# Spectra in 64-row tiles over two banks, the first correlation ahead of the second head sums, and three residual sums on TensorE

## What is computed

```python
Qf = jnp.fft.rfft(Q, axis=2)
Kf = jnp.fft.rfft(K, axis=2)
corr = jnp.fft.irfft(Qf * jnp.conj(Kf), n=Lloc, axis=2)
corr_mean = corr.mean(axis=-1)
w, idx = jax.lax.top_k(corr_mean, top_k)
w = jax.nn.softmax(w, axis=-1)
rolled = jnp.take_along_axis(V[:, :, None, :, :], shifted[..., None], axis=3)
out = jnp.einsum('bhk,bhkld->bhld', w, rolled)
return out @ Wo + bo
...
x = x + jnp.tanh(g_xattn[1]) * _L1_xattn_ref(_layernorm(x, axis=-1), ctx_1024, ...)
x = x + jnp.tanh(g_ffn[1]) * _L1_ffn_ref(_layernorm(x, axis=-1), w_gate, w_up, w_down)
```

## Time and profile before

| | us |
|---|---|
| runs | 276.53, 276.31, 274.62 |
| median | 276.31 |
| profiled execution, in all | 276.65 |
| its span (first to last instruction) | 274.8 |
| PE busy | 253.9 (92%) |
| DVE busy | 190.7 (69%) |
| ACT busy | 164.6 (60%) |
| POOL busy | 131.0 (48%) |

### The profile page before, as it was taken

One profiled execution on the slowest core, in us unless ns is written; L12 is line 12 of the kernel. 1 busy time (PEld: TensorE's weight loads), 2 busy tenths in 40 slices (PEclk: granted clock), 3 DMA queues, 4 the chain that ended last, 5 costly groups with the idle time before them and its releaser, 6 DMA issues.

```text
span 274.8 us, 6251 instructions
## 1 busy us (share of the span) xinstructions
PE 253.9 (92%) x2152; PEld 196.4 (71%) x2152; DVE 190.7 (69%) x494; ACT 164.6 (60%) x384; POOL 131.0 (48%) x207
## 2 busy tenths in 40 slices
PE   8999999999899989999999999979998784989886
PEld 6655376666577868999999999665785442766675
DVE  3898688888988763253222223885769989999993
ACT  2369985666488654675566667473445793354453
POOL 4566579999402403218992220275066633353230
PEclk9999999999999998999999999999999999799999
DMA  6999000000000209776777771000000000000111
GB/s 191 379 348 403 13 4 2 2 4 0 2 2 4 76 20 377 300 289 265 296 300 291 292 290 63 2 1 1 4 0 0 0 0 2 0 19 23 38 39 38
DMA packets 12191, 30.11 MB, mean 110 GB/s; under 512 B 1024, under 2 KB 5248, under 8 KB 12032
## 3 DMA queue, kind: packets, MB, share of 16 engines
q1 hardware_dynamic: 12160, 29.71, 28.5%
HBM read 9.71 MB, written 1.05 MB: 39 GB/s over the span
## 4 chain that ended last, share of the span: by engine, by line
PE 64%; DVE 20%; issue 7%; ACT 5%; POOL 2%; DVEq 0%; POOLq 0%
PE ps L1403 12%; PE ps L1414 12%; PE ps L1252 6%; DVE s_region L294 4%; PE ps L1226 4%; PE ps L1239 4%; PE ps L1159 3%; DVE s_region L1090 3%; PE ps L1542 3%; PE ps L1150 2%; DVE s_small L1095 2%; PE ps L1262 2%; PE ps L1151 2%; PE ps L1344 2%; DVE s_small L237 2%
## 5 line engine op out<-in xcount | busy, mean ns | idle before, releaser
L631 ACT ACTIVATE s_region<-ps,s_region 128x128 f32<-128x128 f32 x144 | 40.8, 371 | 21.8 <-PE ps L1403 21.8
L960 DVE SCALAR_TENSOR_TENSOR s_ctxT<-ps,s_region,s_ctxT 128x64 f32 x72 | 18.1, 281 | 43.8 <-PE ps L1414 43.8
L1403 PE MATMUL ps<-s_region 128*128 128x128 f32 x288 | 38.0, 276 | 0.3 <-issue 0.3
L1414 PE MATMUL ps<-s_region 128*128 128x128 f32 x288 | 37.9, 275 | 0.0
L1403 PEld LDWEIGHTS ps<-s_region 128*128 128x128 f32 x288 | 34.9, 192 | 0.7 <-issue 0.7
L1414 PEld LDWEIGHTS ps<-s_region 128*128 128x128 f32 x288 | 35.0, 192 | 0.2 <-issue 0.2
L420 POOL COPY s_region<-s_xt 128x64 f32 x72 | 14.8, 234 | 32.3 <-PE ps L1403 24.5
L574 ACT COPY s_region<-ps 128x512 f32<-128x512 f32 x32 | 17.2, 592 | 16.2 <-PE ps L1239 16.2
L830 DVE TENSOR_REDUCE s_small<-ps 128x16 f32<-128x1024 f32 x16 | 19.6, 1224 | 9.7 <-PE ps L1226 9.7
L1599 PE MATMUL ps<-s_region 128*128 128x352 f32 x64 | 21.1, 469 | 5.3 <-DVE s_region L1090 3.7
L301 POOL TENSOR_TENSOR s_region<-s_region,s_small 128x704 f32<-128x704 f32 (+2 forms) x11 | 14.6, 1330 | 22.0 <-DVE s_region L294 21.7
(11 more groups left out here) (230 smaller groups left out, 528.7 us busy)
## 6 DMA issues: line engine op xcount, KB each, us to landing
s_region<-s_wall SPq DMA_DIRECT2D x36, 514.0 KB, 3.0
s_wall<-wall SPq DMA_DIRECT2D x8, 514.0 KB, 9.3
s_par<-par SPq DMA_DIRECT2D x1, 1280.0 KB, 10.5
s_x<-x SPq DMA_DIRECT2D x2, 512.0 KB, 6.8
out<-s_x SPq DMA_DIRECT2D x6, 128.0 KB, 1.8
s_region<-ffn SPq DMA_DIRECT2D x1, 560.0 KB, 3.6
s_ctxT<-ctxT SPq DMA_DIRECT2D x2, 256.0 KB, 4.0
s_ctxT<-ctxT SPq DMA_DIRECT2D x1, 512.0 KB, 6.7
```

The source lines that it names most:

```text
L631: ins = act.activation(hg[j % 3][:, c, :], ps[:, j % 3, RPT * S * c:RPT * S * (c + 1)], ACT.Gelu, bias=wbuf[j % 6][:, FF + FC * D + c:FF + ...
L960: dve.scalar_tensor_tensor(row, ps[:, 4 + j % 2, S * k:S * k + S], w, row, ALU.mult, ALU.add).then_inc(m["acc_done"], 1)
L1403: ins = mm(ps[:, j % 3, RPT * S * c:RPT * S * (c + 1)], w[:, P * c:P * c + P], xg[j % 4], start=True, stop=True)
L1414: ins = mm(ps[:, 4 + j % 2, 0:RPT * S], w[:, FF + D * c:FF + D * c + D], hg[j % 3][:, c, :], start=(c == 0), stop=(c == FC - 1))
```

## The change

The matmuls of `spectrum(q)` become those of `spectra(n)`, n = 0 to 3, four tiles a call. For each tile there are two matmuls with 64 contraction rows and 128 columns, one on the array's rows 0 to 63 and one on rows 64 to 127, into two different banks; the zero half of the table is left out. A bank now holds one half u of four tiles, and `roll_values(q)` and `values_added(q)` work on the half q % 2 of group q // 2, with as many elements as before.

`correlate(0)` is issued ahead of `sum_heads(1)`. Group 1's sum with x goes the way of groups 2 and 3 (identity matmul, scaled copy, statistics from PSUM, copy by ScalarE), and the identity matmuls are called `residual(g)` and stand one step earlier. The banks of the out tokens change. VectorE does rolls 6 and 7 before `attention_out(0)`; POOL does their additions before the powers of group 0; ScalarE does `y1_turned(2)` before it normalises group 0.

```diff
-OUT_BANK = (5, 1, 7, 6)
+OUT_BANK = (2, 3, 5, 7)
...
             def values_added(q):
                 pool.wait_ge(m["of_done"], q + 1)
-                straight, swapped = (of[:, z, 2 * q:2 * q + 2, :].rearrange("p t (u c s) -> p (t u) c s", u=2, c=2) for z in range(2))
+                n, u = q // 2, q % 2
+                straight, swapped = (of[:, z, 4 * n:4 * n + 4, S * u:S * u + S].rearrange("p t (c s) -> p t c s", c=2) for z in range(2))
...
             for q in range(1, 6):
                 values_added(q)
-            powers(pool, 0, 4)
             values_added(6)
             values_added(7)
+            powers(pool, 0, 4)
...
-                ins = act.copy(dst, ps[:, 4, :]) if g < 2 else act.activation(dst, ps[:, 4, :], ACT.Identity, scale=tg[:, 2:3])
+                ins = act.copy(dst, ps[:, 4, :]) if g < 1 else act.activation(dst, ps[:, 4, :], ACT.Identity, scale=tg[:, 2:3])
...
             def sum_kept(g):
-                act.wait_ge(m["x3_read"], g - 1)
+                act.wait_ge(m["x3_read"], g)
...
             y1_turned(1)
+            y1_turned(2)
...
+            act.wait_ge(m["x3_done"], 1)
             normalise(act, 0, 4, m["xn_d"], 11, blocked=True)
-            y1_turned(2)
+            sum_kept(1)
+            y1_turned(3)
+            act.wait_ge(m["x3_done"], 2)
             x_magnitude(0)
-            y1_turned(3)
             normalise(act, 4, 8, m["xn_d"], 12, blocked=True)
...
             def roll_values(q):
...
-                dve.wait_ge(m["g_done"], q + 1)
-                rows = slice(4 * q, 4 * q + 4)
-                gps = ps[:, SPEC_BANK[q % 4], :].rearrange("p (t z w) -> p z t w", t=2, z=2)
...
+                n, u = q // 2, q % 2
+                dve.wait_ge(m["g_done"], n + 1)
+                gps = ps[:, SPEC_BANK[q % 4], :].rearrange("p (t z w) -> p z t w", t=4, z=2)
...
-            attention_out(0)
             roll_values(6)
             roll_values(7)
-            attention_out(1)
+            attention_out(0)
+            sum_stats(1)
             x_scale(0)
...
             def turn_weights(g):
                 pe.wait_ge(m["wq_ready"], 1)
-                pe.wait_ge(*((m["wq_used"], 1) if g == 2 else (m["kv_used"], 2 * G4)))
+                pe.wait_ge(*((m["wq_used"], 1) if g == 2 else (m["x3_done"], g + 1)))
...
             turn_sums(0)
+            correlate(0)
             sum_heads(1)
-            correlate(0)
             turn_sums(1)
...
-            def spectrum(q):
-
-                pe.wait_ge(m["gx_ready"], q // 2 + 1)
-                if q >= 4:
-                    pe.wait_ge(m["of_done"], q - 3)
...
-                for k in range(2):
-                    ins = mm(ps[:, SPEC_BANK[q % 4], 2 * P * k:2 * P * k + 2 * P], gx[q // 4][:, lag_index(2 * q + k)].rearrange("p h d -> p (h d)"),
-                             rolled, start=True, stop=True)
+            def spectra(n):
+
+                pe.wait_ge(m["gx_ready"], n + 1)
+                if n >= 2:
+                    pe.wait_ge(m["of_done"], 2 * n - 2)
...
+                table = rolled.rearrange("p (z u w) -> p u z w", z=2, u=2)
+                for k in range(4):
+                    lags = gx[n // 2][:, lag_index(4 * n + k)].rearrange("p h d -> p (h d)")
+                    for u in range(2):
+                        rows = slice(S * u, S * u + S)
+                        ins = mm(ps[:, SPEC_BANK[2 * (n % 2) + u], P * k:P * k + P].rearrange("p (z w) -> p z w", z=2),
+                                 lags[rows], table[rows, u], start=True, stop=True)
                 ins.then_inc(m["g_done"], 1)
...
+            def residual(g):
+                pe.wait_ge(m["bo_added"], g + 1)
+                if g == 1:
+                    pe.wait_ge(m["kv_used"], 2 * G4)
+                elif g == 2:
+                    pe.wait_ge(m["gx_ready"], 4)
+                else:
+                    pe.wait_ge(m["of_done"], 8)
+                mm(ps[:, OUT_BANK[g], :], ident, x[:, 4 * g:4 * g + 4, :].rearrange("p t d -> p (t d)"), start=True, stop=False)
```

More of the change, by code:

```diff
@@ L1025, in roll_values @@
                 dve.wait_ge(m["kv_used"], G4 + q // 2 + 1)
-                dve.wait_ge(m["g_done"], q + 1)
-                rows = slice(4 * q, 4 * q + 4)
-                gps = ps[:, SPEC_BANK[q % 4], :].rearrange("p (t z w) -> p z t w", t=2, z=2)
-                v = vf[:, rows].rearrange("p (t u) c s -> p t (u c s)", u=2).unsqueeze(1).broadcast_to([P, 2, 2, P])
-                dve.tensor_tensor(of[:, :, 2 * q:2 * q + 2, :], gps, v, ALU.mult).then_inc(m["of_done"], 1)
+                n, u = q // 2, q % 2
+                dve.wait_ge(m["g_done"], n + 1)
+                gps = ps[:, SPEC_BANK[q % 4], :].rearrange("p (t z w) -> p z t w", t=4, z=2)
+                v = vf[:, 8 * n:8 * n + 8].rearrange("p (t u) c s -> p u t (c s)", u=2)[:, u].unsqueeze(1).broadcast_to([P, 2, 4, S])
+                dve.tensor_tensor(of[:, :, 4 * n:4 * n + 4, S * u:S * u + S], gps, v, ALU.mult).then_inc(m["of_done"], 1)
             dve.tensor_scalar(bo1g, pc("bo1"), tg[:, 2:3], None, ALU.mult).then_inc(m["bo_scaled"], 1)
@@ L1061, in sum_stats @@
                 ins.then_inc(m["x3_read"], 1)
-                dve.wait_ge(m["x3_read"], g - 1)
+                dve.wait_ge(m["x3_read"], g)
                 aggregate(dve, 4 * g, 4 * g + 4)
@@ L1551, in out_product @@
                 ins.then_inc(m["y1_done"], 1)
+            def residual(g):
[7 more added lines that the diff above has]
+                mm(ps[:, OUT_BANK[g], :], ident, x[:, 4 * g:4 * g + 4, :].rearrange("p t d -> p (t d)"), start=True, stop=False)
             def out_tokens(g):
                 if g == 0:
-                    pe.wait_ge(m["gx_ready"], 4)
-                else:
-                    pe.wait_ge(m["of_done"], 6 if g == 1 else 8)
-                if g >= 2:
-                    pe.wait_ge(m["bo_added"], g + 1)
-                    mm(ps[:, OUT_BANK[g], :], ident, x[:, 4 * g:4 * g + 4, :].rearrange("p t d -> p (t d)"), start=True, stop=False)
+                    pe.wait_ge(m["kv_used"], 2 * G4 - 1)
                 pe.wait_ge(m["y1_ready"], g + 1)
-                mm(ps[:, OUT_BANK[g], :], pc("idft_o"), y1[g % 2].rearrange("p a b -> p (a b)"), start=(g < 2), stop=True).then_inc(m["o_done"], 1)
+                mm(ps[:, OUT_BANK[g], :], pc("idft_o"), y1[g % 2].rearrange("p a b -> p (a b)"), start=(g == 0), stop=True).then_inc(m["o_done"], 1)
             turn_lags(0)
             context_kv(7)
-            spectrum(0)
-            spectrum(1)
+            spectra(0)
             turn_lags(1)
-            spectrum(2)
-            spectrum(3)
-            spectrum(4)
+            spectra(1)
+            spectra(2)
             out_product(0)
-            spectrum(5)
+            spectra(3)
+            residual(1)
             out_tokens(0)
-            spectrum(6)
             out_product(1)
-            spectrum(7)
+            residual(2)
             out_tokens(1)
             out_product(2)
+            residual(3)
             out_tokens(2)
```

3 lines of the change are left out of this document (1 added, 2 removed).

## The result

| | before | after |
|---|---|---|
| median, us | 276.42 | 281.27 |
| runs, us | 274.62 to 276.57 (4) | 280.77 to 281.58 (4) |
| span of the profiled execution | 274.8 | 279.7 |
| ratio, with 95% interval | | 1.017 [1.014, 1.021] |

The account below looks back on a forecast made before the run. The start of pair 0's product (221.16 us) was taken to set the end. Lateness of 0.5, then 0, 0.85 and 1.0 us, carried to the end, gave 277.65, or 277.3 after taking off 0.34; range 275.2 to 279.0.

Parts of the forecast that it names:

- Step 1: First correlation issued ahead of the second head sums: everything up to the lag weights 0.5 us late, bounds 0.45 and 0.71.
- Step 2: Spectra in row tiles, pairs running at once, 1.04 us a call: first out product level with before, lateness 0.
- step 3: Fourth spectra call and group 1's residual ahead of the first out tokens: first attention sum 0.85 us late.
- rival of turns: Row tiles run one after the other, 1.78 us a spectra call: 279.9 us; chance 0.10.
- fixed cost for each small matmul: Each small spectra matmul costs 0.025 us more, 0.2 a call, +0.4 in all: 277.7 us; chance 0.08.
- Step 4: ScalarE's turned product 2 ahead of group 0's normalisation: +0.15 us net, so VectorE's scaling of group 0 is 1.0 late.
- Step 5: Rest of the diff, from group 0's scaling to pair 0's product: unchanged at 10.76 us, so 0 added.
- VectorE as the limit: VectorE's saved work in 205 to 213 us brings group 0's scaling 0.8 us earlier: 275.5 us; chance 0.15.
- Correlation free: Moving the first correlation costs 0 at best, if ScalarE reaches the first exponential before the second copy: 276.8 us; chance 0.06.

Follow-up runs that it names:

- b1: The kernel before with only the first correlation put ahead of the second head sums; 277.99 us, ratio 1.004 [0.998, 1.009].

## Why the prediction was wrong

**What bounds the kernel** was read rightly: the start of pair 0 sets the end, and nothing gave a shift back (+4.15 net there, +4.6 net at the end).

**Step 1, the correlation, +0.5.** Right in mechanism; the size was 0.66, near its upper bound. I took four records at 0.45, from eight in a run at 0.89; the row with its own duration, 0.71, was the better one. In b1 these four records stand on the path with 0.71 again.

**Step 2, level at out product 0.** Right: its start moved by +0.08 (its end by 0.19, which step 3 counts). Row tiles do run at once, 16 records in 1.16 and 1.09 in the chain. That is what the sum had (1.04) and a little more, 0.05 to 0.12 a call. The single records of after show it too: the two halves of a pair start less than 0.04 us apart, and within a call the pairs follow each other at 0.11 (203.22, 203.33, 203.44), as full-array records of 128 columns do; only the first pair stands 0.21 ahead of the second. So the rival of turns (1.78 a call) is refuted, and so is a fixed cost for each small matmul: what a call has over its columns stands where the form changes. By the page "TensorEngine Tiling (Array Packing)" (Performance Considerations) of the Trainium skill, its overhead read as 25 ns more for each step, a call would have been 1.24 by estimate, above all of these. Its other rule (Key Properties), that different tiles can work in parallel, agrees with these rows.

**Step 3, +0.85 at the first attention sum.** Right in mechanism, 1.27 in size. The four pieces are out product 1.14 (I had 0.89), spectra 1.09 (1.04), residual 1.05 (0.86) and tokens 0.86. The first entry behind a call in row tiles is 0.19 to 0.25 longer than its like elsewhere in the chain. I had put entering and leaving together at 0.15 a call; a call's own excess is 0.2 (1.09 for 0.88 of columns), and the 0.19 to 0.25 come on top, behind it.

**Step 4, +0.15 net, 1.0 at the scaling.** Right (+0.05): the normalisation stands directly behind the scaled copy L677, and VectorE waits for it.

```profile
209.81 0.69 ACT L677 ACTIVATE s_region<-ps,s_small 128x512 f32<-128x512 f32 x1 [2.11 <-PE ps L1557]
...
212.06 0.72 DVE L281 TENSOR_REDUCE s_small<-s_region 128x32 f32<-128x544 f32 x1 [1.64 <-ACT s_region L257]
```

VectorE's wait was 1.64 (1.8 forecast). The runs with the copy and the residual put back show what the sum had assumed: two gates in series, of which only the later counts. The size, 1.32 against 1.0, is the 0.42 missed in step 3, less 0.10 taken too high here.

**Step 5, the rest of the diff at 0: this is the step that failed.** It took the way from the scaling to pair 0 as unchanged, 10.76 us. It was 13.59. Up to the un-scaling it was indeed unchanged (5.57 in both kernels). Then turning x to the first gate record took 1.79 instead of 1.33, and from there to pair 0 5.12 instead of 2.75: 0.46 + 2.37 = 2.83, all of it the half clock.

The sentence that ScalarE's new sum and product copies "are covered" held: behind them the magnitude (L736, 213.99) still waited 0.70 us for VectorE. What step 5 didn't ask is how long TensorE would wait off the path. From the magnitude on ScalarE runs without a break to the copies of the turned weights (L646 of before, L647 of after), which TensorE waits for, so they hang on VectorE's scaling, 1.32 net late. One copy fewer in between (that of product 3, now ahead of the magnitude) gave part of it back: they came at 216.53 instead of 215.37, net 0.82 later. TensorE in turn reached that wait earlier: its out tokens 2 no longer wait for a copy queued behind the normalisation (210.54 against 210.57, net 0.37 earlier), and the turning of the weights (L1435) began at 214.30 against 214.48, net 0.52 earlier. The hole grew from both ends, 0.69 to 2.02. The other hole, up to POOL's un-scaling, grew from 0.57 to 1.08. This account of the holes is read from the two timelines; no run takes its parts one by one. Neither hole is on the path: until 218.5 nothing was lost through them. But with both in place the clock fell, and it fell over 218.5 to 225.3, just where turning, gate and up are the path.

I had named a fall of the clock between 205 and 222 as what would make the prediction wrong, and given it neither a chance nor a price. Before itself falls, from 1.00 to 0.76 in the mean of 233 to 237, behind a stretch (231 to 235) in which TensorE was busy 1.36 of 4.00 us, so the question was there to ask. And the price had a bound: with 3.3 us of matmuls at full clock in the two groups (0.67 and 2.65), half a clock costs up to as much again, so the rival would have read up to 277.3 + 3.3 = 280.6. With the measured 2.8, the 0.3 missed at the scaling, the start's 0.34 and the 0.4 behind pair 0 it comes to 281.1, against 281.27 measured; that sum is made after the fact.

**The sum, mended**: start 0.34, step 1 0.66, steps 3 and 4 0.66 on top (1.32 at the scaling), step 5 2.83, tail 0.4: 4.9.

**The rivals.** VectorE as the limit: no, it waited 1.64 us. Tiles taking turns: no. Fixed cost per matmul: no, pairs start 0.11 apart, and the excess stands at each change of form. Correlation free: no, 0.66.

## What to carry to other kernels

An engine's idle time off the path is not free if it is TensorE's: before taking work off it, letting it reach a wait earlier, or making what it waits for later, look at how long its waits get in the microseconds ahead of a dense stretch, and price that stretch at half clock as a rival. "Nothing changes on the path here" has to be asked for the waits beside the path too. And work that is made shorter pays only if something useful stands where it stood: the same row tiles were worth 0.06 us or 0.50 us at the scaling, depending on one line of order.

## What the runs showed of the hardware

**The clock.** In the stretches read here it was at 1.00 or 0.50, with values between only where a stretch held both. It fell with holes of 2.02 and 1.08 us and 0.52 us of work between (after), and with 1.86 and 0.85 and 0.52 between (before with added work on ScalarE and POOL), each time inside the second hole: at 218.5 in after, and at 216.1 in the other, only 0.3 us into it. It fell once with holes of 0.30 and 1.08, at 221.2, when the gate matmuls had begun (220.34). It did not fall behind one of 1.87 followed by work, nor behind 0.69 and 0.57. That it has two levels here and that idleness is what loses the higher one agrees with the page "TensorE: Matmul & The Clock Gate" (Part 1) of the Trainium skill, by which the throttled state is the default and activity releases it. I had not expected waits this short to do it. That three matmuls of waste take 3 us off a kernel was new to me as well.

**Tile forms.** Eight pairs of 64x128 tiles with 128 columns, 16 records, take 1.09 to 1.16 us, against 1.83 for eight records of 256 columns on the full array, which do the same useful work. The first group behind a change of form is 0.19 to 0.25 us longer than the same group elsewhere (out product 1.14 against 0.89, residual 1.05 against 0.86).

**Open**: which of the two holes counts for how much. With the filling in the first hole alone the one profiled execution fell, and the times of the other nine don't settle what the clock did there.
